# Reordered copies, exponentials and statistics in the attention rounds of a gated cross-attention and mixture-of-experts layer

## What is computed

```python
h = layernorm(x)
q = rope(h @ Wq, pos);  k, v = split(ctx @ Wkv);  k = rope(k, pos)    # 32 heads of 16
x = x + tanh(g0) * (softmax(q k^T / 4) v @ Wout + bout)
h = layernorm(x)
probs = softmax(h @ gate_w.T);  weights, selected = top_k(probs, 6)   # of 16 experts
x = x + tanh(g1) * (sum over the selected of weight * expert_e(h) + shared(h))
# expert: silu(h @ w1_gate) * (h @ w1_up) @ w2, inner width 352
```

## Time and profile before

| quantity | value |
| --- | --- |
| median of 3 runs | 1496.58 us (1493.2 to 1500.42) |
| the profiled execution's own time | 1482.25 us |
| its span | 1480.4 us |
| TensorE busy | 1351.3 us, 91% |
| VectorE, ScalarE, GpSimd busy | 767.8, 564.4, 704.9 us |
| mean granted TensorE clock | 0.955 |

### The profile page before, as it was taken

How to read it: one execution, slowest core, us unless ns; L and a number is a source line. 1 busy time by engine, 2 the same in 40 slices (tenths; PEclk the granted TensorE clock), 3 DMA queues, 4 the chain that set the end, 5 groups by cost and what they waited for, 6 DMA issues and landing times.

```text
span 1480.4 us, 32739 instructions
## 1 busy us (share of the span) xinstructions
PE 1351.3 (91%) x8414; PEld 1152.6 (78%) x8415; DVE 767.8 (52%) x1554; ACT 564.4 (38%) x1366; POOL 704.9 (48%) x1135
## 2 busy tenths in 40 slices
PE   4897889989999837999999999999999999999998
PEld 2565566666666526899999999999999999898997
DVE  4467666665666543444444444444444444256666
ACT  4464666665655602333333333333333333121111
POOL 3556755455444440569353555555455400745543
PEclk8799999998999958999999999999999999999999
DMA  4122323222221344543444444444444343356674
GB/s 190 30 91 77 136 91 130 83 76 98 106 93 66 109 151 155 157 129 103 144 144 145 138 145 145 145 145 145 143 143 126 102 145 89 100 165 203 205 207 144
DMA packets 146858, 190.04 MB, mean 128 GB/s; under 512 B 32531, under 2 KB 99604, under 8 KB 144116
## 3 DMA queue, kind: packets, MB, share of 16 engines
q1 hardware_dynamic: 125108, 99.31, 22.7%
q0 software_dynamic: 21696, 90.06, 17.9%
HBM read 116.80 MB, written 72.50 MB: 128 GB/s over the span
## 4 chain that ended last, share of the span: by engine, by line
PE 78%; ACT 6%; DVE 6%; issue 5%; POOL 2%; SPq 2%; DMA 0%; ACTq 0%; DVEq 0%; POOLq 0%
PE bank L1367 34%; PE bank L1401 19%; PE bank L619 7%; PE bank L644 5%; ACT soft L529 4%; PE bank L1378 3%; PE bank L658 3%; PE bank L626 2%; PE bank L731 2%; PE bank L675 1%; DVE smax L896 1%; DVE c_lo L884 1%; SPq L1188 1%; ACT at_hi L552 1%; POOL w_lo L209 0%
## 5 line engine op out<-in xcount | busy, mean ns | idle before, releaser
L1367 PE MATMUL bank<-w_hi,x_hi 128*128 (+1 forms) x1144 | 289.4, 334 | 20.9 <-DVE x_lo L1442 18.4
L1367 PE MATMUL bank<-w_hi,x_lo 128*128 (+1 forms) x1144 | 277.2, 323 | 0.0
L1367 PE MATMUL bank<-w_lo,x_hi 128*128 (+1 forms) x1144 | 277.1, 323 | 0.0
L205 POOL CAST w_hi<-w_raw 128x352 fp32r<-128x352 f32 x144 | 69.2, 531 | 378.7 <-PE bank L1367 378.7
L1316 ACT ACTIVATE silu<-bank 128x352 f32<-128x352 f32 x143 | 66.5, 465 | 401.9 <-PE bank L1367 401.9
L1458 DVE SCALAR_TENSOR_TENSOR act<-silu,row_w,bank 128x352 f32<-128x352 f32 x111 | 64.4, 580 | 299.4 <-ACT silu L1316 298.9
L1367 PEld LDWEIGHTS bank<-w_hi,x_hi 128*128 128x128 f32 x1144 | 192.9, 189 | 21.2 <-issue 18.5
L1367 PEld LDWEIGHTS bank<-w_lo,x_hi 128*128 128x128 f32 x1144 | 200.1, 189 | 0.0
L1367 PEld LDWEIGHTS bank<-w_hi,x_lo 128*128 128x128 f32 x1144 | 199.7, 189 | 0.0
L529 ACT ACTIVATE soft<-bank,smax 128x128 f32<-128x128 f32 x512 | 146.4, 373 | 103.8 <-DVE smax L896 103.8
L1401 PE MATMUL bank<-w_hi,a_hi 128*128 (+3 forms) x429 | 170.8, 398 | 7.2 <-DVE a_lo L1446 6.7
(11 more groups left out here) (182 smaller groups left out, 2235.0 us busy)
## 6 DMA issues: line engine op xcount, KB each, us to landing
xr<-expert_rows SPq DMA_DIRECT2D x444, 64.0 KB, 1.9
y_rows<-y SPq DMA_DIRECT2D x111, 256.0 KB, 2.0
w_raw<-in_w POOLq DMA_DIRECT2D x18, 1408.0 KB, 6.7
w_raw<-in_w POOLq DMA_DIRECT2D x18, 512.0 KB, 7.7
x_sb<-in_x SPq DMA_DIRECT2D x16, 256.0 KB, 3.5
x_res<-in_x SPq DMA_DIRECT2D x16, 256.0 KB, 2.9
x_rows<-x SPq DMA_DIRECT2D x16, 256.0 KB, 3.0
x_rows<-row SPq DMA_DIRECT2D x16, 256.0 KB, 3.2
```

The lines of the kernel that those rows point to most:

```text
L1367: last = nc.tensor.matmul(to[:, 0:WIDTH], xx[jt][:, d, :], w[d][half][:, cols], start=(d == 0 and xx is x_hi and w is w1_hi), stop=(d == D ...
```

## The change

Five things move; no instruction is added, taken away or made different.

- ScalarE: the two copies of the keys (`k_t`) go from slot 4 to slot 5, where they stand behind the exponentials and the `soft_t` copy of that slot. The copy of the values (`v_one`, slot 7) goes behind the exponentials of slot 7. For that, `attend` is split in two, `attend` and `copy_probs`.
- TensorE: the second half of the output projection (slot 4) goes from directly behind the scores to the end of slot 4, behind the keys' transposes, `probs` and `values`.
- VectorE: the statistics of the next x (`load`, first part) go from slot 3 to slot 1, between `c_lo` and the rotation of the queries. For that the rotations become functions of their own.
- VectorE: `place` goes from slot 6 to slot 7, behind the last maximum and ahead of `normalised_row`.

```diff
@@ ScalarE
+                    attend(at, u)
                     if at(PROJECT) and u == 7:
                         b, j, n = at(PROJECT)
                         act.wait_ge(v_mm, b + 1)
...
-                    attend(at, u)
+                    copy_probs(at, u)
...
-                    if at(PROJECT) and u == 4:
+                    if at(PROJECT) and u == 5:
                         b, j, n = at(PROJECT)
                         act.wait_ge(kt_mm, b + 1)
@@ TensorE
                         score_pair(at, u)
-                    if at(TAIL) and u == 4:
-                        project_out(1, *at(TAIL))
                     if at(PROJECT) and u in (0, 4, 7):
...
                     if at(PROJECT) and u == 3:
                         project(u, *at(PROJECT))
+                    if at(TAIL) and u == 4:
+                        project_out(1, *at(TAIL))
@@ VectorE
             def load(u, b, j, n):
-                if u == 3:
+                if u == 1:
                     dve.wait_ge(x_in[j], 16 * (n + 1))
...
+                    if at(PLACE) and u == 7:
+                        place(*at(PLACE))
+                        if isinstance(at(PLACE)[0], int) and at(PLACE)[0] == BATCHES - 1:
+                            block_table()
                     if at(TAIL) and u == 7:
                         normalised_row(*at(TAIL))
...
                     if at(PROJECT):
                         project(u, *at(PROJECT))
+                    if at(LOAD) and u == 1:
+                        load(u, *at(LOAD))
+                    if at(PROJECT) and u == 1:
+                        rotate_q(at(PROJECT)[0])
+                    if at(PROJECT) and u == 2:
+                        rotate_k(at(PROJECT)[0])
...
-                    if at(PLACE) and u == 6:
-                        place(*at(PLACE))
...
-                    if at(LOAD):
+                    if at(LOAD) and u == 7:
                         load(u, *at(LOAD))
```

More of the change, by code:

```diff
@@ L531, in attend, with copy_probs @@
                     last.then_inc(exp_done, 1)
+            def copy_probs(at, u):
                 of, v = earlier(at, u, 1)
@@ L884, in project, with rotate_q, rotate_k @@
                     v.tensor_tensor(c_lo[:], c_raw[:], c_hi[:].bitcast(F32), ALU.subtract).then_inc(c_lo_done, 1)
-                    dve.wait_ge(q_mm, b + 1)
-                    need(dve, qt_mm, b)
-                    rotate(bank[0][:], q_cos, q_sin, b, q_rot)
-                if u == 2:
-                    dve.wait_ge(k_mm, b + 1)
-                    need(dve, kt_mm, b)
-                    rotate(bank[0][:], k_cos, k_sin, b, k_rot)
+            def rotate_q(b):
+                dve.wait_ge(q_mm, b + 1)
+                need(dve, qt_mm, b)
+                rotate(bank[0][:], q_cos, q_sin, b, q_rot)
+            def rotate_k(b):
+                dve.wait_ge(k_mm, b + 1)
+                need(dve, kt_mm, b)
+                rotate(bank[0][:], k_cos, k_sin, b, k_rot)
             def attend(u, b, j, n):
@@ L1072, in one_round @@
                         gate(u, *at(PLACE), gate_ch)
-                    if at(PLACE) and u == 6:
-                        place(*at(PLACE))
-                        if isinstance(at(PLACE)[0], int) and at(PLACE)[0] == BATCHES - 1:
-                            block_table()
-                    if at(LOAD):
+                    if at(LOAD) and u == 7:
                         load(u, *at(LOAD))
```

## The result

The changed kernel takes 1453.92 us (median of 4 runs, 1452.17 to 1455.77); the kernel before took 1495.93 us beside it (4 runs, 1493.2 to 1500.42). The ratio is 0.9717, with a 95% interval of 0.9689 to 0.9744: 2.8% faster, 42 us. The profiled execution took 1454.81 us with a span of 1452.9 us and a mean granted clock of 0.962, where before it was 1482.25, 1480.4 and 0.955. So the two profiled executions lie 27.4 us apart, the two medians 42.0 us. The forecast for the profiled one was 1450.3 us.

The account below looks back on a forecast made before the run. Bound: TensorE waiting for exponentials before scores, plus lost clock. Nine rounds -26.8, rounds 4 to 6 -8.4, others -2, -1.1, +0.5 make -37.8; falls +5.8 give -32 us: 1496.6 to 1465 us, range 1456 to 1490.

Parts of the forecast that it names:

- The walk through the round: Full-clock round followed from the scores of slot 4: 27.0 us forecast, 1.1 us gained; nine rounds -26.8 us with clock up.
- The two falls: Two clock falls expected in the 15 attention rounds, at 2.9 us each, adding 5.8 us; 0 and 5 as ends.
- rival 3: Clock falls at the waits before the transposes of `xn`, every round; 3.2 us each, up to 1507 us; chance 0.09.
- rounds 4 to 6: Early rounds: `c_lo` freed from 10.70 to 0.41 us, -8.4 us together, with bounds of -3 and -11 us.
- it will again: Round 6: TensorE, which waited 2.14 us for GpSimd's rotation of the queries, would wait for it again.
- the late mean: Second mean ends at 302.0 instead of 300.95 us in the full-clock round; said to cost nothing in round 4.
- Rounds 2 and 3: Early attention rounds, forecast to gain about 1 us each.
- I take the same difference off the median: Last step: the median's 14.3 us above the profiled execution kept constant, so 1496.6 - 32 = 1464.6 us.
- a gain of 1.1 instead of 1.9 us in the round: Full-clock round: next scores come 1.9 us earlier, but transposes of `xn` wait for `xn`, so only 1.1 us is gained.
- 0.68 us at the exponentials of slot 4: Statistics moved to slot 1 let the maximum and exponentials of slot 4 start 0.68 us earlier, at no cost.
- two inputs in SBUF: GpSimd and VectorE share SBUF for instructions with two SBUF inputs: `c_lo` is held, the moved statistics, with one, are not.

Follow-up runs that it names:

- k_keys: The kernel before with only the keys' copies moved from slot 4 to slot 5; 1449.00 us, ratio 0.9692 to before.
- b_again: The kernel before, run once more with no edit; 1494.82 us, ratio 0.9989 to before.
- a_projection_back: The changed kernel with the second half of the output projection put back directly behind the scores of slot 4; 1427.85 us, ratio 0.9564 to before.
- b_keys_value_place: The kernel before with the keys' copies, the values' copy and `place` moved, statistics and projection left in place; 1439.87 us, ratio 0.9639 to before.

## Why the prediction was right, and where it was wrong

**The walk through the round held.** Against the scores of slot 4, whose start is 295.19 us before and 284.54 us after:

| step | before | forecast | measured |
| --- | --- | --- | --- |
| exponentials of slot 4 | +2.56 | +1.88 | +1.88 |
| scores of slot 6 | +6.47 | +4.9 | +4.79 |
| second mean ends | +5.76 | +6.8 | +6.84 |
| root starts | +6.62 | +6.9 | +7.12 |
| `row` starts | +10.90 | +11.2 | +11.46 |
| next scores | +12.28 | +10.4 | +10.21 |
| transposes of `xn` | +13.35 | +12.3 | +12.51 |

No wait before the scores of slot 6, a new one ended by VectorE before the transposes of `xn`, the mean about 1 us later: all there. The root began 0.28 us behind its mean, where I had 0.1, and took 4.14 instead of 4.09 us; so the new wait is 1.17 us, not 0.75, and the round 27.2, not 27.0 us. Over nine rounds that is 2.3 us.

**The two falls came.** I took two at 2.9 us. There are two, at the start of the 7th round and where the 8th begins, and they cost 2.7 us together, by the lengths of 29.1 and 28.0 us against 27.2. This is the mechanism of rival 3, at the place it names: with the two waits (0.50 us, and 1.15 us before 213.98 us) the clock goes down at the transposes of `xn`:

```profile
213.98 0.90 PE L629 MATMUL bank<-const,xn 128*128 128x128 f32 x3 [1.15 <-DVE xn L875]
...
213.00:214.00 1.00, 0.02 (x1) 0.02 (x1) 1.00 (x3) 0.00 (x0) 0.77 (x1) 0.85 0.00 0
214.00:215.00 1.00, 1.00 (x5) 1.00 (x6) 0.53 (x1) 0.00 (x0) 0.70 (x2) 0.50 0.05 21
```

Rival 3 asked for 12 in 15 rounds; it came in two of the nine. The Trainium skill (TensorE: Matmul & The Clock Gate, "A second HAM failure mode: psum-queue depth-cycling") says that short waits between groups of matmuls can make the clock swing. The trace agrees as far as this: it fell in two rounds, and not in seven with the same two waits.

**The early rounds were mis-sized.** For rounds 4 to 6 I had put -8.4 us, with -3 and -11 as bounds. They changed by -2.0, -2.7 and +2.1 us (28.1, 37.2, 33.3 before; 26.1, 34.5, 35.4 after): -2.6 us, just outside the bounds (-3.1 us, just inside, if a round is counted from its first scores). Up to the end of round 5 this is 4.7 us in place of 5.8. `c_lo` was freed as I said, to 0.41 us. But the 7.5 us that TensorE had waited in that round before became 7.08 us of waiting for the rotation of the queries, which stands behind the same splitting on GpSimd. What bounded the round was the splitting; `c_lo` was only the first to stand in its way. The larger miss is round 6, where the step that failed is "it will again": TensorE's wait for the rotation didn't stay at 2.14 us but grew to 4.31, and the round got 2.1 us longer, not 2.6 shorter. Before, GpSimd's scatter, which stands ahead of the splitting, waited for the slots (until 155.49 us). In the changed kernel the slots are there at 147.13 us, but GpSimd is at the root of the late second mean from 145.18 to 148.80 us, and the scatter starts at 149.33. So the late mean had a cost here that I had put at nothing. With the projection put back the wait is 3.09 us and the round 30.1 us. k_keys shows the exchange of round 5 too (5.17 us of waiting, `c_lo` 0.68). Rounds 2 and 3 in return gave 3.9 us, not 2.

So the profiled execution went to 1454.81 us, 4.5 us above my 1450.3. 2.3 us of that are the root and the row, 5.8 us rounds 4 to 6, 1.9 us came back by rounds 2 and 3 and 3.1 us by cheaper falls; the rest, 1.4 us, is behind the fifteenth round.

**The step that put the time outside the range is the last one:** "I take the same difference off the median". The median of before lies 14.3 us above its profiled execution, that of after 0.9 us below its own. The difference was no constant of the measurement. It went with the clock: the profiled execution of before had a mean granted clock of 0.955, the best of all its runs, and the others go down to 0.926; the experts' phase took 914.3 to 918.5 us in every profile, so what is lost is lost in the attention rounds. The change takes away most of what lets the clock fall, and so also falls that the profiled execution happened not to have. Rows could have hinted at it: of nine equal rounds before, two were at 1.00, two at 0.94 and five at 0.89, so the number of falls wasn't fixed, and a median 14 us above the profiled time could mean more of them. At 9.6 us for 0.01 of clock, 14.3 us are 0.015, which puts a run at the median at 0.940; the run of b_again at 1494.61 us has 0.940. Had I taken off the clock's part as well, the forecast would have been 1450 us, from the same sum.

**Which part did it was weighed wrong.** The walk gave the gain to all of the parts together. k_keys has as much with one line, and I had taken the later mean for a price worth paying, a gain of 1.1 instead of 1.9 us in the round. a_projection_back shows that there was nothing to pay for: the scores of slot 6 don't need TensorE cleared of the projection, since with it in its old place they wait 0.44 us, and without the later mean the round is 25.9 us. The statistics I credited with 0.68 us at the exponentials of slot 4, where they save nobody; they are worth 12 us in a_projection_back against b_keys_value_place, mostly by GpSimd's queue.

## What to carry to other kernels

Where the clock falls in some of a row of equal rounds and not in others, don't trust one execution: look at the clock and the time of every run, and count what a removed wait gives in the runs that fell more often. When a change has five parts, try each in the best company as well as alone; the statistics were worth nothing alone and 12 us beside the keys' copies, the kernel with the projection's move alone was 15 us faster, and beside the other parts the same move cost 26 us. Where a queued operation is held by another engine's block of work, ask what else stands behind the same block before counting its time as won.

## What the runs showed of the hardware

- A single wait of 1.6 us of TensorE, in a round in which it is busy in nine tenths of the time, costs 3 us or more through the clock in most rounds: an estimated 21 us in nine rounds between two kernels that differ by one line, and are 60 us apart in all. Pairs of waits with about 1.1 us of small matmuls between were followed by a fall three times in all: in two of nine rounds of the changed kernel (0.5 and 1.15 to 1.18 us) and once in k_keys (0.94 and 0.37 us). In b_keys_value_place TensorE waits 0.45 us before the scores of slot 6 and, some 7 us later, 0.67 to 1.39 us before the transposes of `xn`, and the clock never fell in its nine rounds.
- GpSimd's splitting of weights held some instructions of VectorE and not others. In round 5 of the changed kernel GpSimd is at it from 122.57 to 133.11 us. Within it VectorE's rotation of the keys took its usual time, and `prob` twenty times its own; the last row is `prob` in a later round:

```profile
126.03 0.69 DVE L861 TENSOR_TENSOR k_cos<-bank,sincos 128x512 f32<-128x512 f32 x1 [0.63 <-PE bank L622]
...
283.42 0.24 DVE L975 TENSOR_SCALAR prob<-gexp,grec 128x16 f32<-128x16 f32 x1
```

  The rotation reads a bank of PSUM and one tensor in SBUF. `prob` is of 128x16 only, but both things it reads, `gexp` and the value per partition `grec`, are in SBUF, like both inputs of `c_lo` (10.70 us). What the prediction said of two inputs in SBUF fits `c_lo`. `prob` has only one tensor there, and which property makes it be held, no run here settles. It ended at 133.93 us, 0.8 us behind the splitting: GpSimd went on at 133.08 us, without a pause, with the first sum of the rotation (L429, above), and that one ended at 133.90 us.
- The spread of the times went with the clock where the clock fell often: 26 us between the runs of before beside the experiments (0.926 to 0.953). It was 3.6 and 3.8 us for the changed kernel (0.962 to 0.965) and a_projection_back (0.968 to 0.971).
